# Two stages' middle steps written as hardware loops, and the routing rows split on GpSimd, in a transformer and state-space kernel

## The chip, the cores and the metric

The kernel runs on one core of one Trainium2 chip, in one launch. The metric is the device time of one execution, in microseconds. Three executions of the kernel before took 746.62, 747.0 and 746.96 us; the median is 746.96 us.

## The reference, cut to what matters

The input `x` is 8 sequences of 512 tokens with 128 channels. Four residual layers follow one another, with all arithmetic in float32:

```python
x = x + attention(layernorm(x))      # one head of 128 channels, softmax over 512 keys, projection
x = x + ffn(layernorm(x))            # mixture of 16 experts
x = x + mamba2(layernorm(x))         # state-space layer: in-projection, conv of 4 taps, scan, gate, out-projection
x = x + ffn(layernorm(x))            # the same experts and weights once more

def ffn(x):
    t = x * rsqrt(mean(x * x) + eps) * scale
    g = t @ gate_w.T + gate_b                    # 16 logits per token
    route = softmax over the 4 largest, 0 elsewhere
    for e in range(16):
        h = t @ w1[e].T + b1[e]
        s = swiglu(h)                            # the linear half is clipped to the constant 7
        acc += route[:, e] * (s @ w2[e].T + b2[e])
    return x + acc
```

The term of this text is the routed bias, the sum over e of `route[:, e] * b2[e]`. The kernel forms it with one matrix product per sequence: the 16 bias rows times the 16 routing weights of each token. Those routing weights laid out as 16 rows by 512 tokens are called the rows here.

## The kernel before, in words

**Stages.** X stays in SBUF for the whole kernel. There are four stages: attention, FFN 1, state-space, FFN 2. Attention and state-space are software pipelines over the 8 sequences. `skewed(eng, step)` runs nine steps, i from -1 to 7. Step i holds parts of sequence i+1 (flag `first`), sequence i (`second`), sequence i-1 (`third`) and sequence i-2 (`fourth`). Each engine has a `step` function of its own for each of the two stages, and calls `skewed` once for each. In the kernel before `skewed` is a Python loop. So every step is written out as instructions, every number of sequence is a constant, and every semaphore is compared with a constant.

**An FFN stage.** It goes over 8 blocks b (one per sequence), each with 8 pairs q of experts. Points in it are named (b, q). For each pair TensorE computes the hidden sums (`hidden`, L1589 to L1591, three products of high and low parts per expert). ScalarE applies the activation (`silu`, L684). VectorE clips and multiplies with the routing weights (`weigh`, L1110). ScalarE and VectorE split the product in a high part (L690) and a low part (L1117). TensorE adds the output product in bank 6 three pairs later (`ffn_out`, L1565 to L1567, with LAG = 3). At q = 3 of each block the sum of the block before is copied out of bank 6 (L704). Then `ffn_out(F, b, 0)` starts the new sum with the routed bias (L1562), for which it waits for `rows_lo` of block b. TensorE's queue is in order, so all that follows waits too.

**The rows.** `load_rows` (SyncE, L303) loads the 16 rows of one sequence three times in one buffer `rows_f`. They are split in high and low parts in `rows_r[:, b]`. Block 0 is split on GpSimd (`rows_split`, L457 and L459). Blocks 1 to 7 are split by a ScalarE copy (`rows_high`, L719) at the end of pair (b-1, 7) and a VectorE subtraction (`rows_low`, L1142) after pair (b, 0). SyncE issues the load for block b+1 after the routing weights of pair (b, 5).

**The late router.** When an FFN stage begins, the routing of the last sequences isn't finished. It is done between the pairs, at places written out by hand in `late_router` of each engine. For sequence 7 that is: statistics on VectorE at (3, 6) (L1009, L1012), nine small operations on GpSimd (`router_chain`, L415 eight times and L430), normalisation on VectorE at (4, 2) (L1018), transposes and logits on TensorE at (4, 5) and (4, 7), and `router_stash` on GpSimd (L435) behind ScalarE's work at (4, 5). Sequence 6 does the same about two and a half blocks earlier, but its `router_chain` ends before or as the stage begins. GpSimd's queue in an FFN stage is `after_first`: the stash of sequence 6, the chain of sequence 7, the stash of sequence 7.

**Code for a number that is not a constant.** The step functions accept a loop variable for i: `wait` compares with an integer or with an expression of the loop variable, and `least` and the tests `isinstance(b, int)` leave out what only the first or last steps need.

Of the kernel before, what the change touches and what calls it, by code (L numbers as in the profile page):

```python
# [6 lines left out]
F32 = mybir.dt.float32  # L7
F32R = mybir.dt.float32r
BF16 = mybir.dt.bfloat16
ALU = mybir.AluOpType  # L10
# [4 lines left out]
NB = 8  # L15
SEQ = 512
NT = SEQ // P
D = 128
NE = 16
# [20 lines left out]
def build(nc, x, w_qkv, w_proj, b_proj, W_in, conv_w, conv_b, dt_bias, A_log, Dskip, norm_w, W_out,  # L40
          ffn_scale, gate_w, gate_b, mlp1_w, mlp1_b, mlp2_w, mlp2_b, out):
    with ExitStack() as ctx:
# [212 lines left out]
                return  # L255
            eng.wait_ge(s, value)

        def skewed(eng, step, before={}):
            for i in range(-1, NB):
                if i in before:  # L260
                    before[i]()
                step(i, i % 2, i < NB - 1, i >= 0, i >= 1, i >= 2)

        LAG = 3

        def done(F):
            return NB if F is F2 else 0
# [6 lines left out]
        def _(eng):  # L274
# [25 lines left out]
            def load_rows(F, dram, b):  # L300
                wait(eng, rows_lo, b + done(F))
                for g in range(3):
                    eng.dma_start(rows_f[g * PSTEP:g * PSTEP + NE, :], dram[b]).then_inc(rows_in, 16)  # L303
# [21 lines left out]
                    elif q == 3:  # L325
                        eng.wait_ge(M["g"], NT * NB)

            def rows_kept(R, b):
                if b == 1:
                    eng.wait_ge(R["kept"], 16 * NT * (NB - 3))  # L330
                elif b == 5:
                    eng.wait_ge(R["kept"], 16 * NT * (NB - 1))
                elif b == 7:
                    eng.wait_ge(R["kept"], 16 * NT * NB)

            def routes(R, F, dram, finish=None):
                for b in range(NB - 3):
                    keep_route(R, dram, b)
                    if b == 2:
                        eng.wait_ge(R["kept"], 16 * NT * (b + 1))  # L340
                        load_rows(F, dram, 0)
                        if F is F1:
                            load_pair(F, dram, 0, 0)
                if F is F2:
                    free(F, 0)
                    load_pair(F, dram, 0, 0)
                for q in range(1, NR):
                    free(F, q)
                    load_pair(F, dram, 0, q)
                for b in range(NB):  # L350
                    for q in range(0 if b else NR, NQ):
                        if (b, q) == (1, 1):
                            keep_route(R, dram, NB - 3)
                        elif (b, q) == (4, 1):
                            keep_route(R, dram, NB - 2)
                        elif (b, q) == (6, 3):
                            keep_route(R, dram, NB - 1)
                        load_pair(F, dram, b, q)
                        if q == 5 and b + 1 < NB:
                            rows_kept(R, b + 1)  # L360
                            load_rows(F, dram, b + 1)
                        if q == 6 and finish and b >= 2:
                            finish(b - 2)

# [8 lines left out]
        def _(eng):  # L373
# [58 lines left out]
            def router_stash(R, b):  # L432
                eng.wait_ge(R["t"], b + 1).then_inc(passed, 1)
                eng.wait_ge(R["t_hi"], b + 1).then_inc(passed, 1)
                eng.tensor_tensor(ffn_lo[:, b, :], tT[:, :], ffn_hi[:, b, :].bitcast(F32),  # L435
                                  ALU.subtract).then_inc(R["stash"], 1)
# [14 lines left out]

            eng.wait_ge(consts, N_CONST)

            def rows_split(F):
                b = 0
                wait(eng, rows_in, 48 * (b + done(F) + 1))
                eng.tensor_copy(rows_r[:, b, :], rows_f[:, :]).then_inc(rows_hi, 1)  # L457
                wait(eng, rows_hi, b + done(F) + 1)
                eng.tensor_tensor(rows_r[PSTEP:PSTEP + NE, b, :], rows_f[PSTEP:PSTEP + NE, :],  # L459
                                  rows_r[PSTEP:PSTEP + NE, b, :].bitcast(F32), ALU.subtract).then_inc(rows_lo, 1)  # L460
                wait(eng, rows_lo, b + done(F) + 1)
# [8 lines left out]

            def step(i, odd, first, second, third, fourth):
                if not first:
                    rows_split(F1)
                if first:
                    ln1_chain(i + 1)
                    add_bias(i + 1)
                if fourth:
                    router_stash(R1, i - 2)
                if third:
                    router_chain(R1, i - 1)  # L480
            skewed(eng, step, before={1: lambda: (late_constants(), ssm_weights()), 2: b2_parts})

            def after_first(R, F):
                router_stash(R, NB - 2)
                router_chain(R, NB - 1)
                router_stash(R, NB - 1)

            after_first(R1, F1)

# [50 lines left out]
            def step(i, odd, first, second, third, fourth):  # L540
                if not first:
                    eng.wait_ge(F1["out"], NQ * NB)
                    rows_split(F2)
                if first:
                    ssm_norm(i + 1)
                if second:
                    weigh(i, odd, 0)
                    ramps(i, odd, 2)
                    ramps(i, odd, 3)
                    weigh(i, odd, 1)  # L550
                if third and first:
                    router_chain(R2, i - 1)
                if second:
                    gate(i, odd, 0)
                    fade(i, odd, 1)
                if fourth:
                    router_stash(R2, i - 2)
                if second:
                    rms(i, 0)
                    weigh(i, odd, 2)  # L560
                    gate(i, odd, 1)
                    fade(i, odd, 2)
                    gate(i, odd, 2)
                    rms(i, 1)
                    rms(i, 2)
                if first:
                    ramps(i + 1, 1 - odd, 0)
                if second:
                    gate(i, odd, 3)
                if first:  # L570
                    ramps(i + 1, 1 - odd, 1)
                if second:
                    rms(i, 3)
            skewed(eng, step)
            router_chain(R2, NB - 2)
            after_first(R2, F2)

# [2 lines left out]
        def _(eng):  # L580
# [133 lines left out]
                    if after_pair:  # L714
                        after_pair(q)

            def rows_high(F, b):
                wait(eng, rows_in, 48 * (b + done(F) + 1))
                eng.activation(rows_r[:, b, :], rows_f[:, :], ACT.Copy).then_inc(rows_hi, 1)  # L719

            def late_router(R, F, b, q):
                if q == 7 and b + 1 < NB:
                    rows_high(F, b + 1)
                if (b, q) == (0, 0) and F is F2:
                    gT_out(NB - 1, NT - 1)
                elif (b, q) == (0, 4) and F is F2:
                    router_out(R, NB - 3, bank(5))
                elif (b, q) == (1, 5):
                    wait(eng, F["back"], done(F) + 1)
                    router_t(R, NB - 2, 5)  # L730
                elif (b, q) == (2, 5):
                    router_exp(R, NB - 2)
                elif (b, q) == (3, 4):
                    router_out(R, NB - 2, bank(5))
                elif (b, q) == (4, 5):
                    wait(eng, F["back"], done(F) + 4)
                    router_t(R, NB - 1, 5)
                elif (b, q) == (5, 3):
                    router_exp(R, NB - 1)
                elif (b, q) == (5, 7):  # L740
                    router_out(R, NB - 1, bank(5))
# [54 lines left out]
                if second:  # L796
                    attn_out(i, 3)

            skewed(eng, step)


            ffn_all(R1, F1)
# [99 lines left out]
            def step(i, odd, first, second, third, fourth):  # L902
# [60 lines left out]
                    router_out(R2, i - 2, bank(5))  # L963
                if first:
                    decays(i + 1, 1 - odd)
            skewed(eng, step)
            ffn_all(R2, F2)


# [1 line left out]
        def _(eng):  # L971
# [165 lines left out]
                    if after_pair:  # L1137
                        after_pair(q)

            def rows_low(F, b):  # L1140
                wait(eng, rows_hi, b + done(F) + 1)
                eng.tensor_tensor(rows_r[PSTEP:PSTEP + NE, b, :], rows_f[PSTEP:PSTEP + NE, :],  # L1142
                                  rows_r[PSTEP:PSTEP + NE, b, :].bitcast(F32), ALU.subtract).then_inc(rows_lo, 1)

            def late_router(R, F, b, q):
                if q == 0 and b:
                    rows_low(F, b)
                if (b, q) == (0, 0) and F is F2:
                    norms(NB - 1, NT - 1)
                elif (b, q) == (0, 1) and F is F2:  # L1150
# [72 lines left out]
                if first:  # L1223
                    prep(i + 1, 4)

            skewed(eng, step)

            def ssm_stats(b, early=False):
                if isinstance(b, int) and b == 0 and not early:
# [132 lines left out]
            def step(i, odd, first, second, third, fourth):  # L1362
# [65 lines left out]
                    router_weights(R2, i - 2)  # L1428
                if not first:
                    weigh(F2, 0, 0)  # L1430
            skewed(eng, step, before={0: lambda: add_sum(F1, NB - 1, 0)})
            ffn_all(R2, F2)
            add_sum(F2, NB - 1, 0)

# [2 lines left out]
        def _(eng):  # L1437
# [249 lines left out]
                if fourth:  # L1687
                    router_parts(R1, i - 2, bank(7), lambda: wait(eng, R1["lg"], i - 1))

            skewed(eng, step)  # L1690

            ffn_all(R1, F1)
            eng.wait_ge(F1["act"], NE * NB)
# [145 lines left out]
            def step(i, odd, first, second, third, fourth):  # L1839
# [73 lines left out]
                    decay_sums(i + 1, 1 - odd)  # L1913
                if fourth and first:
                    router_parts(R2, i - 2, bank(5), lambda: wait(eng, M["gT"], least(NT * i + 3, NT * NB)))
            skewed(eng, step, before={0: first_chunks})
            ffn_all(R2, F2)
            turn_sum(F2, NB - 1, 0)

# [16 lines left out]
```

## Time and profile before

| | |
|---|---|
| median of 3 executions | 746.96 us |
| the profiled execution | 746.62 us |
| its span, first to last instruction | 744.9 us |
| mean granted TensorE clock | 0.996 |
| attention and loading, to about | 124 us |
| FFN 1 | 124 to 320 us |
| state-space | 320 to about 545 us |
| FFN 2 | to the end |

The profile's span leaves out 1.7 us of the execution. The stages run into one another, so their bounds are approximate. TensorE's matrix products are pipelined and the trace models their ends, so one product's duration overlaps the next one's; the pitch from start to start tells the pace. Weight loads (PEld) run beside the products. Idle time of an engine counts only where the engine that ends the stage waits for it.

### The profile page before, as it was taken

What the parts mean: (1) busy time and instruction counts of PE and PEld (TensorE: products, weight loads), DVE (VectorE), ACT (ScalarE), POOL (GpSimd) and SP (SyncE); (2) the same over time, 40 slices, a digit from 0 to 9 for tenths busy, and PEclk for the clock granted to TensorE, in tenths of its full rate; (3) what the DMA queues carried; (4) which work ended last, traced back from release to release, by engine and by line L of the source; (5) the groups of instructions that cost most, each with busy time, mean ns of one, the idle gap of its engine ahead of it and who ended that gap; (6) DMA issues with size and microseconds to landing.
All of it is one profiled execution on the core that took longest, in us unless ns stands there. A gap on an engine that the chain in (4) does not pass through costs nothing. (4 is left out here: it accounts for less than half of the span.)

```text
span 744.9 us, 13019 instructions
## 1 busy us (share of the span) xinstructions
PE 712.4 (96%) x3800; PEld 577.7 (78%) x3800; DVE 627.3 (84%) x1498; ACT 577.0 (77%) x1096; POOL 239.7 (32%) x389
## 2 busy tenths in 40 slices
PE   4999999999999999978999999999989999999997
PEld 3678788788788878757888888888768887887885
DVE  3568887999899899856779999899869999988986
ACT  2667677988988888847787787787668889888884
POOL 2336455000015010005677677677650000500000
PEclk9999999999999999999999999999999999999999
DMA  9000011645465555200000000000036455655661
GB/s 270 2 2 4 4 37 60 227 181 175 170 200 179 176 171 204 86 0 1 2 1 2 4 3 2 9 3 2 31 140 207 176 202 186 206 184 173 222 202 39
DMA packets 29237, 77.19 MB, mean 104 GB/s; under 512 B 4884, under 2 KB 9455, under 8 KB 29167
## 3 DMA queue, kind: packets, MB, share of 16 engines
q1 hardware_dynamic: 29012, 76.36, 30.6%
q8 instruction: 31, 0.51, 0.3%
q14 instruction: 40, 0.32, 0.2%
q10 hardware_dynamic: 154, 0.00, 0.0%
HBM read 73.73 MB, written 2.62 MB: 102 GB/s over the span
## 5 line engine op out<-in xcount | busy, mean ns | idle before, releaser
L684 ACT ACTIVATE s_ring<-ps,b1T 128x512 f32<-128x512 f32 x256 | 172.6, 690 | 37.8 <-PE ps L1591 36.6
L1110 DVE SCALAR_TENSOR_TENSOR s_ring<-s_ring,top_col,r_all 128x1024 f32<-128x1024 f32 x128 | 165.3, 1292 | 23.7 <-ACT s_ring L684 22.6
L1117 DVE TENSOR_TENSOR s_lo<-s_ring,s_hi 128x1024 fp32r<-128x1024 f32 x128 | 156.2, 1220 | 3.0 <-ACT s_hi L690 3.0
L690 ACT ACTIVATE s_hi<-s_ring 128x1024 fp32r<-128x1024 f32 x128 | 135.1, 1056 | 8.0 <-DVE s_ring L1110 7.5
L1565 PE MATMUL ps<-s_hi,w_hi 128*128 128x512 f32 x256 | 102.0, 399 | 2.8 <-DVE s_lo L1117 2.8
L1589 PE MATMUL ps<-ffn_hi,w_hi 128*128 128x512 f32 x256 | 103.9, 406 | 0.0
L1567 PE MATMUL ps<-s_hi,w_lo 128*128 128x512 f32 x256 | 101.3, 396 | 0.0
L1566 PE MATMUL ps<-s_lo,w_hi 128*128 128x512 f32 x256 | 101.2, 395 | 0.0
L1591 PE MATMUL ps<-ffn_hi,w_lo 128*128 128x512 f32 x256 | 101.1, 395 | 0.0
L1590 PE MATMUL ps<-ffn_lo,w_hi 128*128 128x512 f32 x256 | 101.1, 395 | 0.0
L1565 PEld LDWEIGHTS ps<-s_hi,w_hi 128*128 128x128 f32 x256 | 48.1, 188 | 17.4 <-DVE s_lo L1117 6.1
L1591 PEld LDWEIGHTS ps<-ffn_hi,w_lo 128*128 128x128 f32 x256 | 48.0, 188 | 11.9
L1567 PEld LDWEIGHTS ps<-s_hi,w_lo 128*128 128x128 f32 x256 | 48.1, 188 | 11.6
L1566 PEld LDWEIGHTS ps<-s_lo,w_hi 128*128 128x128 f32 x256 | 48.1, 188 | 11.0
L1589 PEld LDWEIGHTS ps<-ffn_hi,w_hi 128*128 128x128 f32 x256 | 48.2, 188 | 10.3
L1590 PEld LDWEIGHTS ps<-ffn_lo,w_hi 128*128 128x128 f32 x256 | 48.1, 188 | 10.3
L501 POOL TENSOR_TENSOR ramp<-upto,dt_a 128x512 f32<-128x512 f32 x32 | 33.0, 1041 | 70.6 <-DVE dt_a L1308 70.6
L435 POOL TENSOR_TENSOR ffn_lo<-tT,ffn_hi 128x512 fp32r<-128x512 f32 x16 | 21.7, 1354 | 92.9 <-ACT ffn_hi L634 92.9
L415 POOL TENSOR_TENSOR rt_small<-rt_mv,eps 128x4 f32<-128x4 f32 x16 | 6.6, 410 | 108.5 <-DVE rt_mv L1012 107.9
L415 POOL TENSOR_TENSOR rt_small<-rt_small,mhalf 128x4 f32<-128x4 f32 x32 | 37.6, 1174 | 2.5
L1269 DVE SCALAR_TENSOR_TENSOR conv_acc<-ps,conv_taps,conv_acc 128x511 f32<-128x511 f32 (+2 forms) x48 | 35.0, 743 | 3.0 <-ACT conv_acc L814 2.8
L1796 PEld LDWEIGHTS ps<-xb_tok,gram 128*128 128x128 f32 x256 | 32.9, 192 | 1.9 <-issue 0.4
(232 smaller groups left out, 1552.2 us busy)
## 6 DMA issues: line engine op xcount, KB each, us to landing
r_all<-route_dram SPq DMA_DIRECT2D x128, 512.0 KB, 4.0
out_dram<-X SPq DMA_DIRECT2D x8, 256.0 KB, 4.4
X<-in_L_attn_a_x_dram SPq DMA_DIRECT2D x1, 1536.0 KB, 10.1
rows_f<-route_dram SPq DMA_DIRECT2D x48, 32.0 KB, 2.9
w_rows<-in_L_ffn_mlp_w_dram SPq DMA_DIRECT2D x1, 1024.0 KB, 6.4
route_dram<-route_cols SPq DMA_DIRECT2D x64, 8.0 KB, 1.5
X<-in_L_attn_a_x_dram SPq DMA_DIRECT2D x2, 256.0 KB, 3.0
in_rows<-in_L_attn_b_W_in_dram SPq DMA_DIRECT2D x1, 384.0 KB
```

The costliest lines, as they stand in the source:

```text
L415: eng.tensor_tensor(o, a, bb, op).then_inc(R["pool"], 1)
L684: eng.activation(s_ring[q % NR][:, e % 2, :], bank(e % 4), ACT.Silu, bias=b1T[:, e:e + 1], scale=ALPHA).then_inc(F["act"], 1)
L690: eng.activation(s_hi[q % NR][:, :, :], s_ring[q % NR][:, :, :], ACT.Copy).then_inc(F["hi"], 1)
L1110: eng.scalar_tensor_tensor(out=s_ring[q % NR][:, :, :], in0=s_ring[q % NR][:, :, :], scalar=top_col[:, 0:1], in1=r_all[q % NR][:, :, :], o ...
L1117: eng.tensor_tensor(s_lo[q % NR][:, :, :], s_ring[q % NR][:, :, :], s_hi[q % NR][:, :, :].bitcast(F32), ALU.subtract).then_inc(F["lo"], 1)
L1269: eng.scalar_tensor_tensor(out=conv_acc[:, j, s:], in0=bank(7 - k)[:, 0:SEQ - s], scalar=conv_taps[:, j, CONV_W - 1 - s:CONV_W - s], in1=c ...
L1565: eng.matmul(bank(6), w2_hi[:, e, :], hi, start=False, stop=False)
L1566: eng.matmul(bank(6), w2_hi[:, e, :], lo, start=False, stop=False)
L1567: mm = eng.matmul(bank(6), w2_lo[:, e, :], hi, start=False, stop=(e == NE - 1))
L1589: eng.matmul(bank(e % 4), w1_hi[:, e, :], ffn_hi[:, b, :], start=True, stop=False)
L1590: eng.matmul(bank(e % 4), w1_hi[:, e, :], ffn_lo[:, b, :], start=False, stop=False)
L1591: eng.matmul(bank(e % 4), w1_lo[:, e, :], ffn_hi[:, b, :], start=False, stop=True).then_inc(F["h"], 1)
```

## The change

There are two edits.

1. `skewed` is replaced by `skew_pairs` on all engines and in both stages. Steps -1 to 2 and step 7 are written out as before. Steps 3 to 6 become a hardware loop of two turns, with two steps in its body, so that the parity of the buffers is a constant. In the body the sequence is a register, and so is each value a semaphore is compared with and each address that depends on the sequence.
2. All rows are split by GpSimd, in `after_first`, between the router's operations that stand there. `rows_high` on ScalarE and `rows_low` on VectorE are gone. SyncE loads the rows of block b just ahead of the routing weights of pair (b, 0).

```diff
-        def skewed(eng, step, before={}):
-            for i in range(-1, NB):
+        def skew_pairs(eng, step, before={}):
+            for i in range(-1, 3):
                 if i in before:
                     before[i]()
-                step(i, i % 2, i < NB - 1, i >= 0, i >= 1, i >= 2)
+                step(i, i % 2, True, i >= 0, i >= 1, i >= 2)
+            with eng.Fori(3, NB - 2, 2) as i:
+                step(i, 1, True, True, True, True)
+                step(i + 1, 0, True, True, True, True)
+            step(NB - 1, (NB - 1) % 2, False, True, True, True)
...
                 for b in range(NB):
+                    if b == 1:
+                        eng.wait_ge(R["kept"], 16 * NT * (NB - 3))
+                    elif b == 5:
+                        eng.wait_ge(R["kept"], 16 * NT * (NB - 1))
+                    elif b == 7:
+                        eng.wait_ge(R["kept"], 16 * NT * NB)
+                    if b:
+                        load_rows(F, dram, b)
                     for q in range(0 if b else NR, NQ):
...
                         load_pair(F, dram, b, q)
-                        if q == 5 and b + 1 < NB:
-                            rows_kept(R, b + 1)
-                            load_rows(F, dram, b + 1)
...
             def after_first(R, F):
+                rows_split(F, 1)
                 router_stash(R, NB - 2)
+                for b in range(2, 4):
+                    rows_split(F, b)
                 router_chain(R, NB - 1)
+                for b in range(4, 5):
+                    rows_split(F, b)
                 router_stash(R, NB - 1)
+                for b in range(5, NB):
+                    rows_split(F, b)
...
-            def rows_high(F, b):
-                wait(eng, rows_in, 48 * (b + done(F) + 1))
-                eng.activation(rows_r[:, b, :], rows_f[:, :], ACT.Copy).then_inc(rows_hi, 1)
...
-                if q == 7 and b + 1 < NB:
-                    rows_high(F, b + 1)
...
-            def rows_low(F, b):
-                wait(eng, rows_hi, b + done(F) + 1)
-                eng.tensor_tensor(rows_r[PSTEP:PSTEP + NE, b, :], rows_f[PSTEP:PSTEP + NE, :],
-                                  rows_r[PSTEP:PSTEP + NE, b, :].bitcast(F32), ALU.subtract).then_inc(rows_lo, 1)
...
-                if q == 0 and b:
-                    rows_low(F, b)
```

`rows_split(F, b)` is the function of before with b as an argument. It waits for the three loads, copies 80x512 (`rows_hi`), and subtracts 16x512 (`rows_lo`).

## Rows read from the trace of the kernel before

**Rows 1.** Windows: stretch, length, busy us (instructions) per engine, clock, DMA share, GB/s.
```profile
125.00:320.00 195.00, 192.25 (x870) 154.44 (x869) 177.03 (x237) 166.06 (x230) 20.19 (x21) 1.00 0.50 171
```
**Rows 2.** Waits: engine line, releaser: us in total, times, longest.
```profile
ACT s_ring L684 <- PE ps L1591: 36.6, 66, 0.9
PE ps L1565 <- DVE s_lo L1117: 2.8, 5, 0.7
```
**Rows 3.** Timeline of PE, one block's start: start us, us, operation.
```profile
207.49 0.40 PE L1589 MATMUL ps<-ffn_hi,w_hi 128*128 128x512 f32 x1
...
210.29 0.60 PE L1574 MATMUL ps<-ident,tT 128*128 128x128 f32 x4
```
**Rows 4.** Timeline of DVE, weighing of pairs (3, 3) and (3, 4).
```profile
208.29 1.28 DVE L1110 SCALAR_TENSOR_TENSOR s_ring<-s_ring,top_col,r_all 128x1024 f32<-128x1024 f32 x1
...
210.62 1.28 DVE L1110 SCALAR_TENSOR_TENSOR s_ring<-s_ring,top_col,r_all 128x1024 f32<-128x1024 f32 x1
```
**Rows 5.** Operations on the tile rows_r: duration ns min/median/max, first and last start.
```profile
L719 ACT ACTIVATE rows_r<-rows_f x14: 615/618/630, 148.7 to 712.6; 80x512 fp32r<-80x512 f32 x14
L1142 DVE TENSOR_TENSOR rows_r<-rows_f,rows_r x14: 680/681/682, 153.1 to 717.0; 16x512 fp32r<-16x512 f32 x14
```
**Rows 6.** Timeline of POOL, the split of block 0.
```profile
115.74 0.61 POOL L457 CAST rows_r<-rows_f 80x512 fp32r<-80x512 f32 x1
116.43 1.26 POOL L459 TENSOR_TENSOR rows_r<-rows_f,rows_r 16x512 fp32r<-16x512 f32 x1
```
**Rows 7.** Timeline of POOL, FFN 1: the router's chain of sequence 7.
```profile
219.77 2.29 POOL L415 TENSOR_TENSOR rt_small<-rt_mv,eps 128x4 f32<-128x4 f32 x1 [50.33 <-DVE rt_mv L1012]
...
231.06 0.20 POOL L415 TENSOR_TENSOR rt_small<-rt_small,ones 128x4 f32<-128x4 f32 x1
231.34 0.20 POOL L430 TENSOR_TENSOR rt_small<-rt_small,rt_mv 128x4 f32<-128x4 f32 x1
```
**Rows 8.** The same chain in FFN 2, its last.
```profile
650.18 1.05 POOL L430 TENSOR_TENSOR rt_small<-rt_small,rt_mv 128x4 f32<-128x4 f32 x1
```
**Rows 9.** The chain of sequence 6, first and last, as FFN 1 begins.
```profile
123.82 0.20 POOL L415 TENSOR_TENSOR rt_small<-rt_mv,eps 128x4 f32<-128x4 f32 x1 [1.63 <-DVE rt_mv L1012]
...
127.74 0.20 POOL L430 TENSOR_TENSOR rt_small<-rt_small,rt_mv 128x4 f32<-128x4 f32 x1
```
**Rows 10.** Timeline of PE, the bias product of block 4, FFN 1 and 2.
```profile
229.05 0.39 PE L1562 MATMUL ps<-rows_r,b_st 80*128 80x512 f32 x1
...
650.40 0.39 PE L1562 MATMUL ps<-rows_r,b_st 80*128 80x512 f32 x1
```
**Rows 11.** Windows around those two products.
```profile
228.00:236.00 8.00, 8.00 (x38) 6.46 (x37) 6.26 (x9) 6.33 (x10) 3.22 (x5) 1.00 0.50 175
649.00:657.00 8.00, 8.00 (x38) 6.50 (x37) 7.91 (x11) 6.38 (x10) 2.16 (x2) 1.00 0.74 236
```
**Rows 12.** Timeline of POOL and DVE, the stash of sequence 7 beside a weighing.
```profile
239.01 2.43 POOL L435 TENSOR_TENSOR ffn_lo<-tT,ffn_hi 128x512 fp32r<-128x512 f32 x1 [7.47 <-ACT ffn_hi L634]
...
240.18 2.33 DVE L1110 SCALAR_TENSOR_TENSOR s_ring<-s_ring,top_col,r_all 128x1024 f32<-128x1024 f32 x1
```
**Rows 13.** Timeline of PE after a wait, as state-space begins; then the window.
```profile
329.25 0.47 PE L1699 MATMUL ps<-uT,tapT 128*128 128x512 f32 x1 [2.62 <-DVE conv_acc L1269]
...
333.67 0.40 PE L1699 MATMUL ps<-uT,tapT 128*128 128x512 f32 x1
...
324.00:332.00 8.00, 4.81 (x18) 3.48 (x17) 5.32 (x12) 6.22 (x10) 0.00 (x0) 0.87 0.00 0
```
**Rows 14.** Waits of PEld, 340 to 540 us, two with named releasers.
```profile
PEld ps L1820 <- DVE gn L1355: 3.4, 12, 0.6
PEld ps L1699 <- DVE uT L1260: 2.2, 7, 0.6
```
**Rows 15.** Page, parts 3 and 6: code transfers; a small transfer's landing.
```profile
q8 instruction: 31, 0.51, 0.3%
...
route_dram<-route_cols SPq DMA_DIRECT2D x64, 8.0 KB, 1.5
```

More of the change, by code:

```diff
@@ L326, in free @@
                         eng.wait_ge(M["g"], NT * NB)
[L328 to L334, printed above, removed]
             def routes(R, F, dram, finish=None):
@@ L452, in _, with rows_split @@
             eng.wait_ge(consts, N_CONST)
-            def rows_split(F):
-                b = 0
+            def rows_split(F, b):
                 wait(eng, rows_in, 48 * (b + done(F) + 1))
@@ L472, in step @@
                 if not first:
-                    rows_split(F1)
+                    rows_split(F1, 0)
                 if first:
@@ L480, in step @@
                     router_chain(R1, i - 1)
-            skewed(eng, step, before={1: lambda: (late_constants(), ssm_weights()), 2: b2_parts})
+            skew_pairs(eng, step, before={1: lambda: (late_constants(), ssm_weights()), 2: b2_parts})
             def after_first(R, F):
+                rows_split(F, 1)
                 router_stash(R, NB - 2)
+                for b in range(2, 4):
+                    rows_split(F, b)
                 router_chain(R, NB - 1)
+                for b in range(4, 5):
+                    rows_split(F, b)
                 router_stash(R, NB - 1)
+                for b in range(5, NB):
+                    rows_split(F, b)
             after_first(R1, F1)
@@ L542, in step @@
                     eng.wait_ge(F1["out"], NQ * NB)
-                    rows_split(F2)
+                    rows_split(F2, 0)
                 if first:
@@ L573, in step @@
                     rms(i, 3)
-            skewed(eng, step)
+            skew_pairs(eng, step)
             router_chain(R2, NB - 2)
@@ L797, in step @@
                     attn_out(i, 3)
-            skewed(eng, step)
+            skew_pairs(eng, step)
             ffn_all(R1, F1)
@@ L965, in step @@
                     decays(i + 1, 1 - odd)
-            skewed(eng, step)
+            skew_pairs(eng, step)
             ffn_all(R2, F2)
@@ L1224, in step @@
                     prep(i + 1, 4)
-            skewed(eng, step)
+            skew_pairs(eng, step)
             def ssm_stats(b, early=False):
@@ L1430, in step @@
                     weigh(F2, 0, 0)
-            skewed(eng, step, before={0: lambda: add_sum(F1, NB - 1, 0)})
+            skew_pairs(eng, step, before={0: lambda: add_sum(F1, NB - 1, 0)})
             ffn_all(R2, F2)
@@ L1688, in step @@
                     router_parts(R1, i - 2, bank(7), lambda: wait(eng, R1["lg"], i - 1))
-            skewed(eng, step)
+            skew_pairs(eng, step)
             ffn_all(R1, F1)
@@ L1915, in step @@
                     router_parts(R2, i - 2, bank(5), lambda: wait(eng, M["gT"], least(NT * i + 3, NT * NB)))
-            skewed(eng, step, before={0: first_chunks})
+            skew_pairs(eng, step, before={0: first_chunks})
             ffn_all(R2, F2)
```

## The prediction

> **What bounds the kernel now.** I looked first at the table of windows, then at the waits, then at timelines of single blocks.
>
> In an FFN stage TensorE is busy 192.25 of 195 us, VectorE 177.03 [rows 1]. Modelled ends can hide gaps, so I checked the pitch. The twelve products of one pair begin at 207.49 us and the next group at 210.29 [rows 3]: 2.80 us a pair, 0.233 us a product. VectorE weighs pairs 2.33 us apart when it is not held up [rows 4], so it has about 0.47 us to spare in each pair, 3.7 us in a block. ScalarE stood idle 36.6 us in 66 places until TensorE delivered, while TensorE waited for VectorE's low part only 2.8 us in 5 places [rows 2]. TensorE is the bound of both FFN stages, and whatever stops it is lost. The important reading is therefore not how much time an engine gains or loses, but whether something reaches TensorE later than it does now.
>
> **Edit 2: the rows.** Removed are 14 ScalarE copies of 0.618 us (8.7 us) and 14 VectorE subtractions of 0.681 us (9.5 us) [rows 5]. By the reading above both lie beside TensorE's products: I put their removal at nothing. At most it gives back the 2.8 us of [rows 2].
>
> Added are 14 splits on GpSimd. One alone takes from 115.74 to 116.43 + 1.26 = 117.69, that is 1.95 us [rows 6]. They now stand in one queue with the router's work, so I went through that queue block by block. Rows 1 are split ahead of everything. Rows 2 and 3 stand behind the stash of sequence 6, half a block or more ahead of their use. Rows 5 to 7 stand behind the stash of sequence 7, which runs at 239.01 to 241.44 [rows 12], and block 5 needs them a whole block after block 4's 229.05 [rows 10].
>
> Rows 4 are different. They are split only after the chain of sequence 7, whose first operation waits for the statistics VectorE makes at (3, 6). SyncE's load is no difficulty: it is issued when pair (3, 3) is weighed, about 210 us [rows 4]. The chain runs from 219.77 to 231.34 + 0.20 = 231.54 in FFN 1 [rows 7] and ends at 650.18 + 1.05 = 651.23 in FFN 2 [rows 8]. TensorE wants rows 4 for the bias product of block 4, which stands at 229.05 and 650.40 [rows 10]. Today that product doesn't need the chain. After the change it does.
>
> Size of the stall: chain's end, 0.05 to the next start, 1.95 for the split, about 0.1 until TensorE starts. FFN 1: 231.54 + 2.1 = 233.64, against 229.05, is 4.6 us. FFN 2: 653.33 against 650.40 is 2.9 us. Together 7.5 us. TensorE is busy 8.00 of 8 us in both windows there [rows 11], so no idle time stands ready to absorb it.
>
> Bounds: the same nine operations took 127.94 - 123.82 = 4.1 us when VectorE was less busy [rows 9], against 11.8 us in [rows 7]. At 4.1 us the split would end at 226 us and there would be no stall. At the upper end the split's two operations are held up themselves. The nearest row is the stash of 2.43 us, of which only some 1.3 is work, beside a weighing of 2.33 us instead of 1.28 [rows 12]; so add about 1.1 us each, 4 to 5 us over both stages. The term lies between 0 and 12, and I take 7.5, because both executions of the chain in the stages were long.
>
> A stopped TensorE may also lose clock. When state-space begins it waited 2.62 us, the granted clock of that window is 0.87, and the twelve products from 329.25 to 333.67 took 4.42 us instead of 12 x 0.233 = 2.80 [rows 13]; that is a stretch at 1.2 instead of 2.4 GHz for 1.6 us more. I count 1.6 for the stall of 4.6 us and half of it for the shorter one: 2.4 us, bounds 0 and 3.2. The Trainium skill says the same in "TensorE: Matmul & The Clock Gate", in its part on the clock gate, where an idle array falls to half rate. By that rule the shorter stall might cost nothing; the sum would then be 0.8 us lower.
>
> The other splits and VectorE: the one pair of rows that shows it is again [rows 12], where GpSimd's 128x512 operation and a weighing delayed each other, 1.05 us for the weighing. A split has one such operation and a shorter copy, and takes 0.681 us away. Net 0.4 to 1.2 us more per block, against 3.7 us to spare. I put it at 0, with bounds -2.8 (all waits of [rows 2] go) and 14 x 1.2 = 17 (nothing hidden).
>
> **Edit 1: the loops.** Eight of eighteen steps run in loops, four per stage. The products and tensor operations are the same. What is new: nearly each wait compares with a register, so a register operation is added for about each. I counted the waits of one step in the code: attention TensorE 37, VectorE 32, ScalarE 46, GpSimd 16; state-space 91, 99, 91, 58. The trace of before has no such operation. Lower bound 0: queued work covers them. Upper bound: the nearest row is the hand-over between two dependent small operations on GpSimd, 231.34 - 231.06 - 0.20 = 0.08 us [rows 7]; if TensorE paid it for every wait, 4 x (37 + 91) x 0.08 = 41 us. A register operation costs only where an engine is held at that wait. Weight loads waited for VectorE in 12 + 7 places in 200 us, eight steps [rows 14], 2.4 per step; x 0.08 x 8 looped steps is 1.5 us. Waits of VectorE and ScalarE on the way to TensorE pay too, so I take double, 3.2 us: near the lower end, since TensorE's idle time is small.
>
> Each loop jumps back once per engine. Lower bound 0: the code is still at hand. Upper: it is fetched again, with TensorE waiting for all of it. One code transfer costs 0.003 x 16 x 744.9 / 31 = 1.15 us, and a small transfer lands in 1.5 us [rows 15], together 2.65 per jump if the time to land is counted on top. For two loops 5.3 us; I take half, 2.6 us. Fewer instructions are loaded in all, but I find no wait of TensorE for code in the stages, so I count no gain.
>
> **Sum.** 7.5 + 2.4 + 0 + 3.2 + 2.6 = 15.7 us on the profiled execution's own 746.62 us (span 744.9 and 1.7 around it): 762.3 us. The median of the three is 0.34 us higher, which is inside their spread; I leave 762.3.
>
> **Rivals.**
>
> A. The chain is ready in time. For it: alone it takes 4.1 us [rows 9], and it is long only because VectorE's operations stand between. Against: VectorE's load in the stage stays as it is, but for 0.68 us a block. Then only the loops count: 746.6 + 3.2 + 2.6 = 752.4.
>
> B. The jumps and registers cost much more than I took. For it: 91 waits in a state-space step of about 25 us, on engines that are nearly full (TensorE's weight loads are held up there in many short places [rows 14]); a body of two steps may also need more than one transfer. With the stall of 9.9, two jumps of two transfers each in full (10.6 by [rows 15]) and registers at twice my value (6.4) the time is 773.5. The Trainium skill speaks for this one: "Advanced Engine Details and Errata", section ISA Cache, gives the engines other than TensorE a buffer of two lines of 256 instructions. By my count VectorE's two state-space steps and their register operations come near 450 instructions, which can touch three such lines, so the jump would fetch again; no row here shows it.
>
> C. Other side: VectorE, not TensorE, sets the FFN pace. For it: 177 of 195 us busy [rows 1]. Its place is the pair; 0.681 us a block comes off the bound, 9.5 us in all, if the splits on GpSimd delay no weighing. With the loops at 5.8, and no stall, 746.6 - 9.5 + 5.8 = 742.9. It decides as soon as a weighing pitch exceeds 2.80 us. Against: 2.33 us [rows 4], and ScalarE waits for TensorE, not the other way [rows 2].
>
> D. Nothing to see: stall absent, loops hidden. 746.6.
>
> **How the numbers follow.** Forecast 0.66 (its own range 754 to 768), A 0.10, B 0.14, C 0.05, D 0.05. The range 751 to 775 leaves out C, D, some of A and the upper part of B, about 2 in 10. A measurement of this kernel can tell about 0.2% (1.5 us) from no change. Faster by more than that: 0.05 (C). Within it: 0.06 (D and a little of A). Slower: 0.89.
>
> **What would show it.** In the changed profile the bias product of block 4 follows GpSimd's subtraction for the rows with an idle TensorE before it of 3 to 5 us in each FFN stage, and the granted clock falls behind at least one. The other bias products have no such wait. ScalarE and VectorE are busy about 8.7 and 9.5 us less, GpSimd some 27 us more. The middle steps of attention and state-space take 0.2 to 1 us longer each, with a gap on some engine at the jump. The prediction is wrong if block 4's product isn't late (then A or D), if the looped steps are over 2 us longer each (B), or if the FFN blocks get shorter than their products at 0.233 us each (C).

## The result, and the profile after

| | before | after |
|---|---|---|
| median | 746.98 us (4 runs) | 764.6 us (4 runs, 763.29 to 765.02) |
| the profiled execution | 746.62 us | 764.16 us |
| its span | 744.9 us | 762.4 us |
| mean granted TensorE clock | 0.996 | 0.984 |

The ratio is 1.0228, interval 1.0207 to 1.0249: 2.3% slower. The forecast was 762.3 us.

**Where the time is lost.** I compared the start times of the same product in both traces: the logits of the last attention step, the bias product of each FFN block, and state-space's decay sums of each sequence (the sum of sequence n stands in step n - 1). The later of two adjacent differences, less the earlier, is what that stretch lost.

| product | start after less start before, us |
|---|---|
| attention logits, last | 0.74 |
| FFN 1 bias product, blocks 0 to 7 | 0.73, 0.73, 0.73, 0.72, **3.62, 5.24**, 5.44, 5.36 |
| state-space decay sums, sequences 0 to 7 | **6.57**, 6.56, 6.56, 6.28, 6.66, 6.78, **13.20**, 13.33 |
| FFN 2 bias product, blocks 0 to 7 | 12.74, 12.73, 12.73, 12.73, **15.66, 17.29**, 17.52, 17.52 |

The last value is also the difference of the spans, 762.4 - 744.9 = 17.5. So nearly all of it was lost at a few places (in us): before block 4's bias product in each FFN stage (2.9 and 2.9), right behind it (1.6 and 1.6), at the start of state-space (1.2), and between the decay sums of sequences 5 and 6, where the loop jumps back from step 4 to step 5 (6.4). Attention has 0.9: its first logits, ahead of the loop, are 0.14 early, its last 0.74 late.

**Block 4.** First GpSimd in FFN 1 in the kernel after (timeline: start us, us, operation): the end of the chain and the split, which answer to [rows 6, 7]. L435 was L430, L461 and L463 were L457 and L459.

```profile
220.56 1.09 POOL L420 TENSOR_TENSOR rt_small<-rt_mv,eps 128x4 f32<-128x4 f32 x1 [25.07 <-issue]
...
230.44 0.20 POOL L435 TENSOR_TENSOR rt_small<-rt_small,rt_mv 128x4 f32<-128x4 f32 x1
230.58 0.61 POOL L461 CAST rows_r<-rows_f 80x512 fp32r<-80x512 f32 x1
231.26 1.26 POOL L463 TENSOR_TENSOR rows_r<-rows_f,rows_r 16x512 fp32r<-16x512 f32 x1
```

Then TensorE at the same place (L1560 was L1562), which answers to [rows 10].

```profile
229.53 0.40 PE L1589 MATMUL ps<-ffn_hi,w_lo 128*128 128x512 f32 x1
232.67 0.47 PE L1560 MATMUL ps<-rows_r,b_st 80*128 80x512 f32 x1 [2.74 <-POOL rows_r L463]
...
234.93 0.63 PE L1587 MATMUL ps<-ffn_hi,w_hi 128*128 128x512 f32 x1
235.36 0.63 PE L1588 MATMUL ps<-ffn_lo,w_hi 128*128 128x512 f32 x1
...
237.55 0.40 PE L1564 MATMUL ps<-s_lo,w_hi 128*128 128x512 f32 x1
237.79 0.40 PE L1565 MATMUL ps<-s_hi,w_lo 128*128 128x512 f32 x1
```

The split follows the chain at once, and TensorE starts 0.15 us after the split's end. Behind the wait products stand 0.43 us apart (235.36 - 234.93), and at 237.55 again 0.24. The windows say the same (after the length: busy us and instructions of PE, PEld, DVE, ACT and POOL, then the granted clock, DMA share, GB/s). The first line answers to [rows 11], the other two are the 3 to 4 us behind each stall, at about half of full speed, which is 1.2 GHz.

```profile
228.00:236.00 8.00, 5.26 (x19) 3.91 (x18) 7.08 (x8) 3.58 (x5) 4.21 (x6) 0.86 0.39 135
...
234.00:237.00 3.00, 3.00 (x8) 2.31 (x7) 1.45 (x2) 0.55 (x1) 0.00 (x0) 0.50 0.53 162
667.00:671.00 4.00, 4.00 (x13) 3.12 (x12) 1.84 (x2) 0.77 (x2) 0.00 (x0) 0.57 0.50 166
```

The operations on the tile `rows_r` (durations in ns: min/median/max) answer to [rows 5], with who waited for the tile. TensorE has two stalls, 5.5 us together, and no other bias product waits. (The 50.1 us are GpSimd's own idle time ahead of the chain.) A split that takes 0.61 + 1.26 us when alone takes 1.35 + 1.71 us in the median.

```profile
L461 POOL CAST rows_r<-rows_f x16: 607/1350/2391, 116.5 to 724.7; 80x512 fp32r<-80x512 f32 x16
L463 POOL TENSOR_TENSOR rows_r<-rows_f,rows_r x16: 1257/1710/2152, 117.2 to 725.5; 16x512 fp32r<-16x512 f32 x16
...
who waited for it (us, times):
  POOL rt_small L420: 50.1, 2
  PE ps L1560: 5.5, 2
```

**The jump in state-space.** Timeline of VectorE where the loop jumps back, in the kernel after.

```profile
477.53 0.23 DVE L1073 TENSOR_TENSOR rt_w<-rt_tmp,rt_sum 128x64 f32<-128x64 f32 x1
480.77 0.87 DVE L1231 BATCH_NORM_STATS2 ln_st<-X 128x6 f32 x4 [3.01 <-issue]
```

L1073 is the end of the body, L1231 its beginning, and "issue" means that VectorE waited for nothing that the profile shows. A wait of 1.15 us of the same kind follows 2 us later, at L1234. In the kernel before the same two operations follow one another without a gap:

```profile
470.81 0.23 DVE L1068 TENSOR_TENSOR rt_w<-rt_tmp,rt_sum 128x64 f32<-128x64 f32 x1
470.95 0.86 DVE L1233 BATCH_NORM_STATS2 ln_st<-X 128x6 f32<-128x128 f32 x4
```

In the kernel after TensorE then lacks VectorE's work, and its clock falls (timeline of PE, then windows):

```profile
478.80 1.89 PE L1771 MATMUL ps<-ramp,after 128*128 128x512 f32 x4
483.71 0.68 PE L1818 MATMUL ps<-ident,gn 128*128 128x128 f32 x2 [3.02 <-DVE gn L1353]
```
```profile
480.00:482.00 2.00, 0.69 (x2) 0.00 (x0) 0.87 (x4) 0.53 (x2) 0.00 (x0) 1.00 0.07 16
...
485.00:488.00 3.00, 3.00 (x16) 3.00 (x15) 2.66 (x10) 1.89 (x7) 0.49 (x1) 0.50 0.00 0
```

The DMA view of 476 to 485 us shows what moved meanwhile:

```profile
q14 instruction: 3, 0.02, 0.9%
```

Three code transfers of 8 KB. The other code queue, q8, has 16 KB a transfer and none here. That VectorE waited for these is so far a reading by their place in time: the kernel before, too, has two q14 transfers from 468 to 480 us and no wait. e4, e6 and e7 test it. The attention loop shows no such gap.

**What the edits freed.** From the page after: the engines' busy times, and the two VectorE operations of each pair (L1110 and L1117 before).

```profile
PE 721.4 (95%) x3800; PEld 583.5 (77%) x3800; DVE 630.8 (83%) x1484; ACT 571.0 (75%) x1082; POOL 281.3 (37%) x417
...
L1115 DVE SCALAR_TENSOR_TENSOR s_ring<-s_ring,top_col,r_all 128x1024 f32<-128x1024 f32 x128 | 168.8, 1320 | 30.2 <-ACT s_ring L695 29.7
L1122 DVE TENSOR_TENSOR s_lo<-s_ring,s_hi 128x1024 fp32r<-128x1024 f32 x128 | 161.3, 1260 | 3.0 <-ACT s_hi L701 3.0
```

And the same lines of the page before:

```profile
PE 712.4 (96%) x3800; PEld 577.7 (78%) x3800; DVE 627.3 (84%) x1498; ACT 577.0 (77%) x1096; POOL 239.7 (32%) x389
...
L1110 DVE SCALAR_TENSOR_TENSOR s_ring<-s_ring,top_col,r_all 128x1024 f32<-128x1024 f32 x128 | 165.3, 1292 | 23.7 <-ACT s_ring L684 22.6
L1117 DVE TENSOR_TENSOR s_lo<-s_ring,s_hi 128x1024 fp32r<-128x1024 f32 x128 | 156.2, 1220 | 3.0 <-ACT s_hi L690 3.0
```

VectorE does 14 subtractions of 0.681 us less, 9.5 us, and is busy 3.5 us more. Its two operations per pair took 3.5 + 5.1 = 8.6 us longer in all. ScalarE is busy 6.0 us less, GpSimd 41.6 us more.

### The profile page after: what moved, and what is told of

Read it like the earlier page. It is cut to its first block and busy times, and to the rows that moved or that the text cites. A ratio compares the mean times of both kernels' runs of the same rounds, so it can differ in the third digit from the quotient of the medians.

```text
span 762.4 us, 13642 instructions
## 1 busy us (share of the span) xinstructions
PE 721.4 (95%) x3800; PEld 583.5 (77%) x3800; DVE 630.8 (83%) x1484; ACT 571.0 (75%) x1082; POOL 281.3 (37%) x417
## 5 line engine op out<-in xcount | busy, mean ns | idle before, releaser
L1115 DVE SCALAR_TENSOR_TENSOR s_ring<-s_ring,top_col,r_all 128x1024 f32<-128x1024 f32 x128 | 168.8, 1320 | 30.2 <-ACT s_ring L695 29.7
L1122 DVE TENSOR_TENSOR s_lo<-s_ring,s_hi 128x1024 fp32r<-128x1024 f32 x128 | 161.3, 1260 | 3.0 <-ACT s_hi L701 3.0
L461 POOL CAST rows_r<-rows_f 80x512 fp32r<-80x512 f32 x16 | 21.0, 1310 | 141.9 <-DMA rows_f<-route_dram 141.9
L440 POOL TENSOR_TENSOR ffn_lo<-tT,ffn_hi 128x512 fp32r<-128x512 f32 (+1 forms) x16 | 20.6, 1284 | 66.5 <-ACT ffn_hi L645 66.5
```

Of the source, the lines that this page charges most:

```text
L1115: eng.scalar_tensor_tensor(out=s_ring[q % NR][:, :, :], in0=s_ring[q % NR][:, :, :], scalar=top_col[:, 0:1], in1=r_all[q % NR][:, :, :], o ...
L1122: eng.tensor_tensor(s_lo[q % NR][:, :, :], s_ring[q % NR][:, :, :], s_hi[q % NR][:, :, :].bitcast(F32), ALU.subtract).then_inc(F["lo"], 1)
```

## The experiments

Each ratio is against the kernel before on the same chip, with its interval. Edits are told against the changed kernel, except in e9.

**e1, the rows alone.** All steps written out, rows on GpSimd as changed.

```diff
-            for i in range(-1, 3):
+            for i in range(-1, NB):
                 ...
-            with eng.Fori(3, NB - 2, 2) as i:
-                ...
```

> The changed kernel with all steps of both stages written out; only edit 2 (rows split on GpSimd) is left. My theory: the block-4 bias product still waits for the chain, about 2.9 us in each FFN stage, and the half-rate clock behind it adds 1.6 each, so 747 + 9 = 756 us. Rival (the loops carry most of the loss, and the two stalls only show because the stages are shifted): below 751. Rival (GpSimd's splits hold up weighings in every block): also about 756, but the blocks other than 4 are longer than before.

Measured: 755.08 us, 1.0109 (1.0082 to 1.0135). Block 4's product came 2.9 us late in both stages, and in its trace the clock fell only behind the second. Waits of TensorE in FFN 1:

```profile
PE ps L1552 <- POOL rows_r L455: 2.7, 1, 2.7
```

The stall belongs to the rows and needs no loop.

**e2, the loops alone.** `skew_pairs` kept; `rows_high`, `rows_low` and the load at pair 5 as before.

```diff
-                for b in range(2, 4):
-                    rows_split(F, b)
...
+                if q == 7 and b + 1 < NB:
+                    rows_high(F, b + 1)
...
+                if q == 0 and b:
+                    rows_low(F, b)
```

> The kernel before with the middle steps of both stages as hardware loops; only edit 1 is left. My theory: VectorE waits about 3 us for its code at the jump back in the state-space stage, TensorE loses about 6.4 us there with the clock, attention costs 0.7 us, so 747 + 7 to 8.5 = 754 to 755.5 us, and the steps away from the jump are as long as before. Rival (register operations cost in each looped step): the same sum, but each of the four state-space steps 1.5 us longer.

Measured: 754.67 us, 1.0092 (1.0071 to 1.0114). No stall at the bias products; between the decay sums of sequences 5 and 6 it lost 6.4 us, as the changed kernel. VectorE's waits of that kind, of which 3.04 and 2.02 us stand at the jump:

```profile
DVE ln_st L1241 <- issue: 5.5, 4, 3.0
```

VectorE's two operations per pair stay at 1290 and 1218 ns, so their slowing comes from the rows on GpSimd, not from the loops. The two parts cost 8.1 and 6.9 us by their ratios, the whole 17.0: 2 us more than the sum. The trace of the whole has two costs that neither part's trace has: 1.6 us of clock behind block 4 in FFN 1, and 1.2 us of the longer stretch at half clock as state-space begins (0.93 granted from 320 to 345 us in both, 0.80 in the whole). Times differ within a few us from one execution to the next, so this is no exact account.

**e3, rows 4 ahead of the chain of sequence 7.**

```diff
-                for b in range(2, 4):
+                for b in range(2, 5):
                     rows_split(F, b)
                 router_chain(R, NB - 1)
-                for b in range(4, 5):
-                    rows_split(F, b)
```

> The changed kernel with the split of rows 4 moved ahead of the router's chain of sequence 7 in GpSimd's queue; nothing else. My theory: both stalls and both clock falls behind them go, 764.5 - 9 = 755.5 us. Rival (the splits cost by holding up VectorE's weighings, whatever their order): 762 us or more. A third way: the chain itself now comes later and VectorE's normalisation waits instead, 759 to 762 us.

Measured: 757.09 us (753.38 to 758.15, 5 runs), 1.0135 (1.0114 to 1.0157), 1.6 us more than I expected. TensorE waits for no rows any more. The wait has a new place: in FFN 1 VectorE's normalisation of (4, 2) waited 2.3 us for the chain (1.7 before, 0.4 in the changed kernel), since the split of rows 4 now stands ahead of it, and blocks 5 and 6 lose 1.3 us together.

The trace is of the fastest of the five executions, 753.38 us, and the only one whose clock stayed at 1.00 throughout. It shows what the jump costs without the clock. VectorE waits as in the changed kernel:

```profile
476.43 0.87 DVE L1229 BATCH_NORM_STATS2 ln_st<-X 128x6 f32 x4 [3.04 <-issue]
478.48 0.38 DVE L1232 BATCH_NORM_AGGREGATE ln_mv<-ln_st 128x2 f32<-128x6 f32 x4 [1.17 <-issue]
```

Between the decay sums of sequences 5 and 6 it lost 3.9 us instead of 6.4. So some 2.5 of the 6.4 are the clock that fell behind the wait.

**e4, VectorE's state-space steps written out**, on the other engines the loops stay.

```diff
-            skew_pairs(eng, step, before={0: lambda: add_sum(F1, NB - 1, 0)})
+            skewed(eng, step, before={0: lambda: add_sum(F1, NB - 1, 0)})
```

> The changed kernel, but on VectorE alone the state-space steps are written out; the other engines keep their loops. My theory: the stall at the jump is VectorE's code fetch alone, so 764.5 - 6.4 = 758 us, and no wait of 3 us stands at the middle of the stage. Rival (every engine pays for the jump, or register waits cost): 762 to 764.5 us, with another engine late at the same place.

Measured: 756.92 us, 1.0142 (1.011 to 1.0174), 6.4 us under the changed kernel by the ratios. Between the same decay sums only 0.5 us are lost instead of 6.4. VectorE's longest wait between 476 and 502 us is now 0.3 us:

```profile
DVE cb L1319 <- PE ps L1770: 0.3, 1, 0.3
```

The jumps of TensorE, ScalarE and GpSimd are still there and cost nearly nothing. The price is VectorE's jump alone. The code queue q14 carries 35 transfers here against 39 in the changed kernel (and 40 in the one before), though VectorE's code is longer now: the jump cost more transfers than the two steps that it saves.

**e5, rows on GpSimd without loops and without the late product** (e1 and e3 together).

> All steps written out as before; the splits of rows 1 to 7 on GpSimd as in the change, but rows 4 are split ahead of the chain of sequence 7. No loops and no late bias product are left, so only what the splits save ScalarE and VectorE, and what they disturb, can show. Theory (VectorE and ScalarE lie beside TensorE's products in the FFN): the time is the time before, about 747 us, within 1.5. Rival C (VectorE sets the FFN pace, so 0.681 us come off per block): 9.5 us less, about 737.5. If the splits delay weighings beyond what is to spare (the 17 us bound): 750 or more, with TensorE waiting for VectorE in the FFN blocks. e3, with loops, stood 2.4 us behind at block 5 of FFN 1 though nothing was waited for at block 4, so a small loss of up to 2 us is possible.

Measured: 749.32 us (12 runs), 1.003 (1.0014 to 1.0046). Rival C would have had 737.5. The edit frees ScalarE and VectorE and still costs 2 us. The trace is of the fastest execution, 747.11 us; it has no half clock as state-space begins and gains 1.5 us there. Blocks 5 and 6 of FFN 2 lose 1.8 us; the waits of VectorE and TensorE between 650 and 700 us say why:

```profile
DVE t L1013 <- POOL rt_small L427: 2.3, 1, 2.3
```
```profile
PE ps L1553 <- DVE s_lo L1112: 1.8, 3, 1.2
```

VectorE waited for the chain, fell behind, and TensorE waited for the low part. Its operations per pair took 1336 and 1271 ns, against 1292 and 1220 before: 128 x 0.095 = 12 us more, for 9.5 us taken off.

**e6, the state-space loop with one turn**: steps 3 and 4 in registers, 5 and 6 written out, no jump back.

```diff
+            with eng.Fori(3, 5, 2) as i:
+                step(i, 1, True, True, True, True)
+                step(i + 1, 0, True, True, True, True)
+            for i in (5, 6):
+                step(i, i % 2, True, True, True, True)
```

> The changed kernel, but the state-space loop makes one turn, over steps 3 and 4, and steps 5 and 6 are written out: the same two register-steps without any jump back. Theory (the jump back is the price: VectorE waits 3.0 + 1.2 us for its code, and TensorE's clock halves behind it): the 6.4 us between decay sums 5 and 6 go, the time is about 758, and steps 3 and 4 keep the length that they have in the changed kernel. Rival (register operations and register-valued waits cost, not the jump): only half of what the loop costs goes, about 761, and steps 3 and 4 are longer than the written-out steps 5 and 6. Rival (the time is lost wherever VectorE's steps reach new code, looped or not): no change, about 764.5.

Measured: 756.02 us, 1.0111 (1.0088 to 1.0134), 8.7 us under the changed kernel by the ratios; I had 6.4, and the profiled executions, 764.16 and 757.61 us, differ by 6.6. The one of e6 is the slowest of its four, with the lowest clock. In its trace the decay sums stand 5.73, 6.15, 6.24, 6.23, 6.23 us behind those of before for sequences 3 to 7. So the two steps in registers lose 0.4 and 0.1 us, and the 6.4 are gone. Register operations are nearly free; the jump is the price.

**e7, the changed kernel with a hint**: VectorE's state-space loop names the target of the jump ahead of it.

```diff
-            with eng.Fori(3, NB - 2, 2) as i:
+            with nc.Fori(3, NB - 2, 2, engines=[eng.engine], hint_back_edge=True) as i:
```

> The changed kernel, but VectorE's state-space loop tells the engine ahead of the jump where it goes (the hint for the back edge). Theory (VectorE waits 3.0 + 1.2 us for code behind its jump): if the hint makes the fetch early, the waits shrink and the time is about 758; the two 8 KB code transfers come before the jump. Rival (the stall is no code fetch but something else at the jump, such as the register compare or a pipeline drain): no change, about 764.5. Third outcome: the hint comes too near the jump to hide anything, or the two steps don't fit in what the engine holds, and the loss stays with the transfers a little earlier.

Measured: 760.95 us, 1.0179 (1.0156 to 1.0202): 3.7 us back, not 6.4. At the jump VectorE waited 0.6 us instead of 3.0 + 1.2, and no code transfer of q14 falls between 476 and 485 us. But the wait came again where the loop is left, with three code transfers beside it (timeline of VectorE, then of TensorE):

```profile
546.21 0.18 DVE L1031 BATCH_NORM_AGGREGATE rt_mv<-rt_st 128x2 f32<-128x6 f32 x1 [2.66 <-issue]
```
```profile
547.51 0.68 PE L1794 MATMUL ps<-skip_diag,xs 128*128 128x128 f32 x4 [1.91 <-DVE y L1352]
```

A stall that goes from the jump when the jump is announced, and comes back at the exit beside code transfers, is best read as a fetch of code; the trace doesn't record the fetch as what VectorE waits for. VectorE also waited 1.2 us as it entered the loop, and the steps behind got 0.4 us longer each; why is open.

**e8, e3 and e7 together.**

> The changed kernel with rows 4 split ahead of the chain of sequence 7, and VectorE's hint at the state-space jump. Theory: both losses go, 764.5 less 9.0 (two stalls of 2.9 and the clock behind them, 1.6 each) less 6.4 is about 749. If the hint does nothing: as e3, 753 to 758. If the two parts that are left (attention loops 0.8, longer half clock at the start of state-space 1.2) were all there is: not under 747.5. A time below 746.5 would say that the freed ScalarE and VectorE are worth something.

Measured: 754.33 us, 1.0097 (1.0074 to 1.0121), 5 us over my 749. The sum had no term for the exit (2.4 us of waiting here) nor for e5's loss.

**e9, the kernel before with loops in attention alone.**

> The kernel before with nothing but the attention stage's middle four steps in loops, on all engines. The changed kernel's attention starts its steps 0.1 to 0.4 us later each, 0.8 us in all, with no gap behind the jump. Theory (register operations and the attention jump cost next to nothing): 0.8 us more than before, about 747.8, and state-space and the FFN stages are as before. Rival (register operations cost 0.08 us at each wait where an engine is held, as I had put it; 1.6 us for attention and its jump another 1.3): about 749.9.

Measured: 747.88 us (12 runs), 1.0005 (0.9993 to 1.0018). In the trace FFN 1 starts 1.7 us behind, of which 0.7 to 0.8 were there in the first steps, before any loop; the loop itself has 0.9. As expected, and by the ratio not to be told from nothing (the medians are 1.2 us apart, 747.88 and 746.66).

**e10, e3 and e4 together.**

> The changed kernel with rows 4 split ahead of the chain of sequence 7 and VectorE's state-space steps written out, so without the late bias product and without VectorE's jump. Theory (the losses add up): 764.6 less 7.5 (what rows 4 ahead of the chain gave in the middle of the earlier runs) less 7.7 (what writing out gave) is 749.4, at most 751; with the profile of rows on GpSimd and no loops at 749.3 this leaves 0 to 1.5 us for every loop that is left. Rival (the two overlap, since both end in the same wait for a late VectorE or a lower clock): 752 or more. A time under 746.5 would mean that a loop or the freed engines save something after all.

Measured: 752.5 us (747.0 to 753.38, 8 runs), 1.0066 (1.0044 to 1.0087). That is 1.5 us above the upper end I gave, and the rival's side. In its trace FFN 2 loses 4.3 us between blocks 3 and 6: VectorE waits 2.3 us for the chain again, TensorE 1.8 us for the low part, and this time its clock falls (windows of 6 us; the clock is the third number from the end):

```profile
688.00:694.00 6.00, 4.21 (x18) 2.97 (x16) 5.97 (x7) 3.88 (x6) 0.97 (x1) 0.93 0.40 136
694.00:700.00 6.00, 6.00 (x23) 4.79 (x22) 5.06 (x5) 3.97 (x7) 0.00 (x0) 0.79 0.57 186
```

No version of either edit beats the kernel before; e9 comes nearest.

## Why the prediction was right, and which terms were not

The forecast of 762.3 us was 2.3 us under the median, and its chief mechanism is the one seen. That the sum came so near is in part luck: the stall was put 1.7 us too high, the clock 2.0 us too low, and loops and jumps 1.7 to 2.0 us too low, the last by two errors in opposite directions. Measured by the start times above, against the sum of 15.7 us:

| term | predicted | measured | shown by |
|---|---|---|---|
| stall at block 4, both stages | 7.5 | 2.9 + 2.9 = 5.8 | trace after, e1, e3 |
| clock behind it | 2.4 | 1.6 + 1.6 = 3.2, and 1.2 as state-space begins | trace after |
| splits against VectorE | 0 | 0 in this trace, some 2 by e5 | e5 |
| register operations | 3.2 | 0.9 in attention, 0.2 to 0.5 in state-space (to the sums of sequence 5, from those of sequence 0 or 3) | trace after, e6, e9 |
| jumps | 2.6 | 6.4, of which some 2.5 is the clock behind the wait (e3) | e3, e4, e6, e7 |

**The stall** was right in cause and place. The size in FFN 1 was 1.7 us too large: the chain ran 10.1 us (220.56 to 230.64) instead of 11.8 [rows 7], and block 4 itself was due 0.73 us later. In FFN 2 the 2.9 us were met exactly: there the chain ran 10.1 us in the kernel before, too. The signs I gave had TensorE idle for 3 to 5 us; it was 2.74 and 2.77. The 4.1 us of rival A [rows 9] were in neither stage. The undoing (e3) shows the cause but gives back less than the stall and its clock, because rows 4 ahead of the chain make VectorE wait for the chain. In FFN 1 of the kernel before VectorE had waited 1.7 us for it already. I had looked at who waits for the rows, and not at who waits for the chain.

**The clock.** I gave the shorter stall half the price; both cost 1.6. In e1 and e4 a stall of the same length cost nothing in FFN 1 and 1.6 in FFN 2. So a wait of 2.7 us lies where the fall comes in one execution and not in another. By the rule I named from the Trainium skill ("TensorE: Matmul & The Clock Gate", the part on the clock gate) the shorter stall might have cost nothing; it did so in FFN 1 of e1 and e4 and not in the changed kernel. For a wait at the jump I had no clock term at all, and it took some 2.5 us.

**The splits.** The net of 0 was right in this trace: but for the places named, no FFN block is over 0.3 us longer. The working behind it was not. I expected 0.4 to 1.2 us more of VectorE's time per block, hidden in what it has to spare; its two operations per pair took 8.6 us more in 16 blocks, against 9.5 taken off, about 0.1 us less per block. My list of signs contradicted that working: it had VectorE busy 9.5 us less, as if no split delayed it, and it was busy 3.5 us more. GpSimd was busy 41.6 us more instead of 27, because I had sized the split by the one that ran alone [rows 6]. And the loss in e5's trace came by the wait for the chain, a way that I hadn't looked at. The Trainium skill gives the rule in "SBUF — State Buffer", section SBUF: two separate sides: a VectorE operation with two inputs in SBUF and a GpSimd operation that reads there hold one pair of ports in turn. The durations above agree with it (1220 to 1260 ns for the subtraction with two SBUF inputs). Rival C is refuted by e5: with no stall and no loop the time is over that of before.

**Registers and jumps** failed in opposite directions and made up for each other in part: predicted 5.8 together, measured 7.5 to 7.8. My guess of a hand-over of 0.08 us paid at a few places per step was too dear; that work queued ahead covers it is likely, but no run shows it. The step that failed is the pricing of the jump as a transfer hidden by half: 2.6 us for both loops, where one alone cost 6.4. I took the 16 KB transfers of q8 as the measure and asked whether TensorE waits for code. It isn't seen to, and no q8 transfer falls into the stretch of the jump. The wait is VectorE's, beside 8 KB transfers of q14, 3.0 + 1.2 us, and TensorE's next product hangs on it. Rival B had that mechanism, "a body of two steps may also need more than one transfer", at 10.6 us for two jumps; it was one jump at 6.4, and the rival's other half, the registers, did not come. Its sign, looped steps over 2 us longer each, is met by the step with the jump and by no other. The ISA Cache section of "Advanced Engine Details and Errata" in the Trainium skill speaks of two lines; a body whose head is gone at the jump (after) and whose exit is gone when the head is fetched early (e7) agrees with so small a store. By that section a line has 16 KB; the q14 transfers here have 8 KB each. I had priced attention's jump like the other, and it cost nothing that can be seen.

**Open** stays why the half clock as state-space begins lasted 3.4 us before (329.9 to 333.3), 10.2 us after (329.3 to 339.5), and was absent in e3, e5, e8 and e10, where the granted clock from 320 to 345 us is 1.00. The wait that goes ahead is 2.6 us in the kernel before, e2, e3, e5, e8 and e10 alike; in the kernel after the clock had fallen ahead of that wait. The long stretch stands in the traces of the kernel after, e6 and e7 alone, the same three whose clock fell behind block 4 in FFN 1; e1 and e4, where it didn't, have the short one. Whether the one leads to the other no run tests. It moves the time by up to 3 us either way, and is in the spread of e5 and e10.

## What to carry to other kernels

When an operation is moved into the queue of another engine, look not only at whether its own consumer is late, but at who waits for what now stands behind it (e3 and e5 both lost there), and size it by its duration beside its neighbours, not alone. Before rolling a pipeline into a loop, ask engine by engine whether the body stays in the engine's code store: the one engine that must fetch at the jump stops all that wait for it. A hint for the jump gave back 3.7 us here, and the wait came again at the exit. An engine relieved by 9.5 us is worth nothing if the work taken off slows it by as much from where it went.

## What the runs showed of the hardware

- At the one jump back over VectorE's long state-space body it waits 3.0 + 1.2 us (after, e3) or 3.0 + 2.0 us (e2), beside 8 KB code transfers; TensorE loses 3.9 us at full clock (e3) and 6.4 us where the clock falls behind the wait (after, e2). The jumps of the other engines cost 0.5 us at most (e4), and at the attention jump no such gap is seen.
- Values in registers, for waits and addresses, added 0.1 to 0.4 us to a state-space step of 27.3 us (after, e6).
- GpSimd's 80x512 copy took 0.61 us alone and up to 2.39 beside VectorE (after).
- A wait of TensorE of about 2.7 us was followed by 3 to 4 us at 1.2 GHz in some executions (cost 1.6 us; both stages of the kernel after) and by none in others (FFN 1 of e1 and e4).
